# GpSimd in place of VectorE subtracts the hi half of the core path's gelu

## The reference, cut to what matters

```
h = x @ down_w + down_b
gate, topi = top-2 of softmax(x @ router_w + router_b - 1e-7 * cost)
out = sum over the 2 chosen of 8 experts: gate * (gelu(gelu(h) @ w1 + b1) @ w2 + b2)
out = out + 0.1 * (gelu(gelu(h) @ shared_w1 + shared_b1) @ shared_w2 + shared_b2)
out = out @ up_w + up_b
out = out + (gelu(x) @ core_w + core_b)      # the core path
```

## Time and profile before

| | us |
|---|---|
| median of 3 runs | 806.69 (806.05 to 808.78) |
| the profiled execution | 806.75 |
| its span, first to last instruction | 805.0 |
| PE busy | 780.5 |
| DVE busy | 684.9 |
| ACT busy | 628.5 |
| POOL busy | 440.9 |

### The profile page before, as it was taken

The page is one execution under the profiler, slowest core; times in us unless marked ns, Lnnn a source line. Parts: engine busy times, 40 slices in busy tenths (PEclk is TensorE's granted clock), DMA queues, the critical chain, the costliest instruction groups (busy, mean ns, idle before and its releaser), DMA issues.

```text
span 805.0 us, 14397 instructions
## 1 busy us (share of the span) xinstructions
PE 780.5 (97%) x4742; PEld 696.0 (86%) x4742; DVE 684.9 (85%) x1713; ACT 628.5 (78%) x1417; POOL 440.9 (55%) x305
## 2 busy tenths in 40 slices
PE   7899999999999999999999999999999889989997
PEld 6689898999999999999999999999999767778786
DVE  4789898888888888888888888889999988887967
ACT  3787878878788788887788888788788968776974
POOL 2555355664446655455566544576445464578654
PEclk9999999999999999999999999999999999999999
DMA  7263233343222344322244332244322131112221
GB/s 254 76 171 69 62 92 93 92 103 88 66 67 66 97 109 108 88 66 67 69 109 106 92 93 66 68 103 129 90 72 66 46 107 49 57 53 67 72 99 53
DMA packets 47593, 70.53 MB, mean 88 GB/s; under 512 B 5536, under 2 KB 38464, under 8 KB 47392
## 3 DMA queue, kind: packets, MB, share of 16 engines
q1 hardware_dynamic: 47008, 68.81, 32.4%
q0 software_dynamic: 368, 0.81, 0.3%
q10 hardware_dynamic: 144, 0.00, 0.0%
HBM read 25.49 MB, written 2.17 MB: 34 GB/s over the span
## 4 chain that ended last, share of the span: by engine, by line
PE 63%; ACT 17%; DVE 11%; issue 5%; POOL 2%; DMA 1%; SPq 0%; DVEq 0%; POOLq 0%
PE M L734 10%; PE M L735 10%; PE M L733 10%; PE T L733 7%; PE T L735 7%; PE T L734 7%; PE S L733 5%; PE S L735 4%; PE S L734 4%; ACT PB L674 3%; ACT PB L625 3%; ACT pth L701 2%; DVE S L1150 2%; ACT qk L687 2%; ACT hh L667 1%
## 5 line engine op out<-in xcount | busy, mean ns | idle before, releaser
L575 POOL TENSOR_TENSOR X<-X,fb 128x512 f32<-128x512 f32 x64 | 83.1, 1298 | 239.0 <-DVE fb L1187 239.0
L582 POOL TENSOR_TENSOR ptl<-ptl,pth 128x640 fp32r<-128x640 f32 x126 | 196.8, 1585 | 26.6 <-ACT pth L701 26.5
L625 ACT ACTIVATE PB<-S,nb 128x384 f32<-128x384 f32 (+3 forms) x256 | 133.3, 534 | 97.0 <-DVE nb L1150 96.9
L674 ACT ACTIVATE PB<-PB,ri 128x256 f32<-128x256 f32 (+3 forms) x256 | 124.5, 580 | 8.8 <-DVE ri L1159 8.8
L1166 DVE STREAM_TRANSPOSE gab<-PB 128x256 f32<-128x256 f32 (+2 forms) x192 | 109.3, 620 | 0.7 <-DMA ptl<-gab 0.7
L1150 DVE CUSTOM_DVE_ANT_0 S<-S,cc 128x384 f32<-128x384 f32 (+2 forms) x192 | 104.8, 575 | 1.0 <-PE S L735 1.0
L1133 DVE TENSOR_TENSOR qk<-M,qk 128x512 fp32r<-128x512 f32 x108 | 74.4, 689 | 20.1 <-ACT qk L687 19.9
L701 ACT CAST pth<-ptl 128x640 fp32r<-128x640 f32 x128 | 88.3, 753 | 1.1 <-DMA ptl<-gab 1.1
L733 PE MATMUL M<-hh,W 128*128 128x512 f32 x222 | 87.0, 392 | 1.3 <-DVE hl L1119 1.3
L735 PE MATMUL M<-hh,W 128*128 128x512 f32 x222 | 87.1, 392 | 0.0
L734 PE MATMUL M<-hl,W 128*128 128x512 f32 x222 | 87.0, 392 | 0.0
(11 more groups left out here) (261 smaller groups left out, 2477.0 us busy)
## 6 DMA issues: line engine op xcount, KB each, us to landing
ptl<-gab SPq DMA_DIRECT2D x256, 160.0 KB, 3.1
stage<-in_wat SPq DMA_DIRECT2D x16, 512.0 KB, 5.0
gab<-scw SPq DMA_DIRECT2D x16, 256.0 KB, 3.2
tmp<-scw SPq DMA_DIRECT2D x16, 256.0 KB, 3.4
X<-in_x SPq DMA_DIRECT2D x3, 512.0 KB, 8.2
stage<-in_wfa SPq DMA_DIRECT2D x3, 512.0 KB, 4.7
out<-X SPq DMA_DIRECT2D x3, 512.0 KB, 2.6
X<-in_wmod SPq DMA_DIRECT2D x1, 1024.0 KB, 11.8
```

The source lines that it names most:

```text
L575: pool.tensor_tensor(X[:, a:a + 512], X[:, a:a + 512], fb[:, c2 * 512:c2 * 512 + 512], ALU.add).then_inc(s_y, 1)
L582: pool.tensor_tensor(ptl[u % 2][:, s], ptl[u % 2][:, s].bitcast(F32), pth[u % 2][:, s].bitcast(F32), ALU.subtract).then_inc(s_pl, 1)
L625: ins = act.activation(PB[:, P_OFF[i]:P_OFF[i] + w], PS[bk][:, a:a + w], ACT.Exp, bias=nb[:, i:i + 1], scale=-1.0, accum_out=sm[:, i:i + 1])
L674: act.activation(p, p, ACT.Copy, scale=ri[:, i:i + 1]).then_inc(s_P3, 1)
```

## The change

The subtraction of `gx` goes from VectorE's loop to GpSimd's. It stands at the same place in the list, which on GpSimd is ahead of the next `hs` (for k = 0) and among the accumulations and powers. It waits for both gelus of ScalarE. As the f32 copy's completion was counted on the semaphore `s_v`, which VectorE uses in order, that gelu now counts on a new one, `s_xf`.

```
+        s_xf = sem("s_xf")
...
 (GpSimd's loop, behind "hs")
+                if ev[0] == "gx":
+                    _, t, k = ev
+                    pool.wait_ge(s_xg, 2 * t + k + 1)
+                    pool.wait_ge(s_xf, 2 * t + k + 1)
+                    hi, lo = gx_at(t, k)
+                    pool.tensor_tensor(lo, stage[:, 512:1024], hi.bitcast(F32), ALU.subtract).then_inc(s_xl, 1)
...
 (ScalarE's loop)
-                    act.activation(stage[:, 512:1024], stage[:, 0:512], ACT.Gelu).then_inc(s_v, 1)
+                    act.activation(stage[:, 512:1024], stage[:, 0:512], ACT.Gelu).then_inc(s_xf, 1)
...
 (VectorE's loop)
-                elif kind == "gx":
-                    _, t, k = ev
-                    xv += 1
-                    v.wait_ge(s_xg, 2 * t + k + 1)
-                    v.wait_ge(s_v, xv)
-                    hi, lo = gx_at(t, k)
-                    v.tensor_tensor(lo, stage[:, 512:1024], hi.bitcast(F32), ALU.subtract).then_inc(s_xl, 1)
```

## The result

| | median us | runs | against before |
|---|---|---|---|
| before | 806.71 | 8 (804.83 to 808.78) | |
| changed | 810.49 | 8 (808.65 to 810.99, and one at 851.12) | ratio 1.0041, 95% interval 1.0025 to 1.0057 |
| forecast | 810.9 | range 807.6 to 812.8 | slower, 0.69 |

In microseconds the ratio is +3.3 (2.0 to 4.6) and the medians differ by 3.8. The run at 851.12 had a granted clock of 0.845 over its span, the other seven 0.989 to 0.994; the ratio leaves it out, and why its clock was low is not known. Measured twice more, the changed kernel had ratios of 1.0031 (1.0018 to 1.0043) and 1.0041 (1.0022 to 1.0059).

The account below looks back on a forecast made before the run. GpSimd was taken to bound the stretch from 700 to 719 us, TensorE what follows. Chain 1.7, held step 1.0, clock 1.3 and tail 0.2 sum to 4.2 us, forecast 810.9 us, range 807.6 to 812.8.

Parts of the forecast that it names:

- GpSimd is the bound from 700 to 719 us: Batch 1 stretch before TensorE's wait for `ur`: GpSimd is busy for all 19.00 us and sets the pace.
- the collision at 713: GpSimd's addition at 713.02, 1.74 us beside VectorE's `gxl`, should take 1.29 with that subtraction moved: -0.45.
- The chain to the power, +1.7: GpSimd's queue up to the power for `rs` 2, 9: added subtractions less gains make it +1.7 us later (0.9 to 2.9).
- The held step, +1.0: Behind `rs` 2, 10: VectorE's L1016 stands still until GpSimd's subtraction of (1,1) ends, +1.0 us (0 to 1.27).
- TensorE at the first gxh matmul, 1.0: Core path's start: TensorE loses 1.0 us waiting for GpSimd's subtraction of (0,1), which costs nothing by itself.
- The clock, +1.3: Behind the `ur` pause, grown from 2.07 to 3.8 us: TensorE's clock falls, costing +1.3 us (0 to 2.3).
- The tail, +0.2: End of batch 3: two more GpSimd subtractions use up its idle time; the rest is +0.2 us (0 to 1.0).
- Batch 2 has nothing near the end: Batch 2: its two subtractions fall into a busy stretch of GpSimd with nothing near its end; no term in the sum.
- The rival: Batch 2 slips too: held router steps make TensorE wait there by 1 to 2 us, 812.5 us; chance 0.14.

Follow-up runs that it names:

- e2: Kernel before with only the subtractions of (0,1) and (1,0) on GpSimd; median +0.96 us, ratio 1.0014 against before.
- e7: Kernel before, subtractions on VectorE, with `hs` and `gx` of batch 1 moved later in the list; median -2.71 us, ratio 0.9954 against before.
- e5: Changed kernel unedited, measured again; median +3.17 us, ratio 1.0031 against before.
- e11: Changed kernel unedited, measured a third time; median +3.09 us, ratio 1.0041 against before.
- e1: Kernel before with only the subtraction of (1,1) on GpSimd; median +0.95 us, ratio 1.0011 against before.
- e6: Changed kernel with GpSimd's subtraction of (1,1) moved behind `acc` 1, 7; median +1.69 us, ratio 1.0021 against before.
- e4: Changed kernel with 48 small matmuls on zeros ahead of TensorE's wait for `ur`; median +2.40 us, ratio 1.0029 against before.
- e8: Changed kernel with `hs` and `gx` of batch 1 moved later in the list; median -1.74 us, ratio 0.9979 against before.
- e10: Changed kernel with 34 small matmuls on zeros ahead of TensorE's wait for `ur`; median +1.70 us, ratio 1.0025 against before.
- e3: Kernel before with only the four subtractions of batches 2 and 3 on GpSimd; median +0.76 us, ratio 1.0002 against before.
- e9: Kernel before with 30 small matmuls on zeros ahead of TensorE's wait for `ur`; median -0.77 us, ratio 0.9994 against before.
- e12: Changed kernel with `hs`, `gx` of batch 1 later and batch 0's two subtractions back on VectorE; median -2.85 us, ratio 0.9973 against before.

## Why the prediction was right, and where it was not

- *GpSimd is the bound from 700 to 719 us.* Right. In e2 GpSimd's two subtractions move its power by 1.56 and TensorE's restart by 1.57, and in e7 the two additions that leave, with the collision at 713, move them by 2.83 and 2.80.
- *The chain to the power, +1.7.* Right in its sum, but partly by luck. From the first instruction behind the gelu to the power it is 718.40 - 694.70 = 23.70, against 22.12: +1.6, and 23.68 in e2. Each subtraction took 1.24, the chain's first accumulation came 0.35 earlier (3.14 behind, against 3.49), and the collision at 713 went (0.45, as forecast). But the powers were mis-sized: 705.12 - 699.86 = 5.26 before, and 705.16 - 699.10 - 1.24 = 4.82 after, so they gained 0.44 where the sum allowed 0.1 at most. They had stood beside VectorE's subtraction of (0,1), which the change removes: the row of three powers is 5.30 in the six profiles that have it on VectorE, and 1.64 and 3.24 in the eight that don't. And one term was missing: a wait of 0.32 for VectorE's L1016, from the starved cast below. The two errors cancel in this profile. In e5 and e11, where the cast got in earlier, the power comes only 1.3 and 1.2 later than before.
- *The held step, +1.0.* The mechanism is shown by e1 and e6; its size is 0.8, as VectorE's row is 0.99 in place of 0.19. The rule of the Trainium skill (SBUF — State Buffer, "Who interferes with whom") had it there, and by the bare row of L1016 it would have been nothing. The runs agree with the rule. One reading that the prediction put beside it was wrong, though: `rs` 2, 10 (L1012, now L1019) is a TENSOR_SCALAR with one input, not two, and so is the cast L1014, and both were held beside a busy GpSimd (1.17 in the profile of before, 3.84 after). The reciprocal, with one input too, was not: it took 0.18 at 720.71, inside the subtraction of 720.61. So two inputs are not the only case that is held.
- *TensorE at the first gxh matmul, 1.0.* Measured 0.91 in this profile, and 2.0 to 2.1 in e2, e4, e5, e6, e8, e10 and e11. In the changed kernel's profile the clock had been low from 690 to 696 us, which made TensorE late there, as in the profile of before from which I had worked; in those seven it had been 1.00. The profile of before:

```profile
692.00:694.00 2.00, 2.00 (x8) 0.76 0.00 0
694.00:696.00 2.00, 2.00 (x6) 0.50 0.00 0
696.00:698.00 2.00, 2.00 (x9) 0.89 0.00 0
```

- *The clock, +1.3.* The fall came (0.55 and 0.60 for 4 us, +1.2 in this execution), so its own price was sized well. But this is the step that was mis-sized as a difference. I compared with a kernel before that keeps its clock, and e3, whose batch 1 is that of the kernel before, has a pause of 3.04 and a low clock behind it. The term is 0.6 by e9 to e11, if it is not nothing.
- *The tail, +0.2.* VectorE's last product did wait for GpSimd (1.74, until 800.30), yet the end moved by less than 0.1 against TensorE's last chunk, partly since it had waited 0.19 for TensorE at the gating before and no longer does.
- *Batch 2 has nothing near the end.* Not quite: a wait of 0.4 for `wgw`, the last router step. VectorE was held in 757 to 759 us there as in batch 1. The rival had put 1 to 2 us on it, the sum nothing.

With the measured sizes the sum is 2.4 + 0.6 + 0.4 + 0.1 = 3.5, or 3.1 with the +2.0 of e11's distance, and the ratios say 3.3, 2.5 and 3.3. The forecast of 4.2 above the kernel before was too high by the clock (0.7), by the chain with the held step (2.7 for 2.0 to 2.4) and by the tail (0.1), and too low by batch 2 (0.4).

## What to carry to other kernels

An engine at 55% of the span can be the bound of a stretch: look for a window in which it has no idle time, and for a chain of waits that stays on it, before giving it more. Work moved onto GpSimd cost twice here, once in its own queue (e2) and once through the VectorE instructions that stand still beside it, even where GpSimd was idle (e1). The cheap cure was not to move work between engines but to move it in the list, out of the bound stretch (e7).

## What the runs showed that I had not expected

**VectorE can starve.** The cast L1014 (128x32) took 3.84 us: it started at 714.28 and ended at 718.12, over three GpSimd instructions that followed each other without a gap (714.30, 715.54, 716.78), and only when GpSimd itself stopped, to wait for the step behind this cast. It took the same 3.84 in e6 and e10, and 1.30, 0.99, 1.00 and 1.26 in e2, e4, e5 and e11, where it got in between two. What decides this is not shown. In the kernel before it was 0.67. It was not on the path but for 0.32 us. The Trainium skill (SBUF — State Buffer, "Who interferes with whom") says that the one who comes first keeps the pair for the whole instruction and the other blocks; here VectorE was blocked over three instructions of GpSimd.

**The clock falls in some executions and not in others.** Behind the pause for `ur` the granted clock went low in all five profiles where it was 2.75 us or longer (after, e1, e3, e6, e11: 3.54, 3.85, 3.04, 2.75, 3.12), and in one (e5, 1.78) of the three with an unfilled pause of 1.8 to 2.4 us. Of the waits of 2.0 to 2.1 at the first `gxh` matmul two of seven were followed by a low clock (e4, e5). And in three profiles (before, after, e12) it was low for some microseconds between 690 and 698 us behind 16 narrow matmuls (128x16), with 0.45 us of idle time ahead of them in the profile of before, where the other eleven kept 1.00. A fall behind the pause for `ur` costs 1.1 to 1.4 us, in e11 2.6, which can be a part of the spread of the kernel before (804 to 810 us); how much of it was not measured.
